# Third attention: scores made a second time by keys, with the row maximum and the mask added by products, and denominators by products with ones

## The chip, the cores and the metric

The kernel is one launch on one core of a Trainium2 chip. The metric is the device time of that launch in microseconds (us); lower is better. The core's engines are TensorE (PE, its weight loads are listed as PEld), VectorE (DVE), ScalarE (ACT), GpSimdE (POOL) and SyncE (SP, which issues transfers). Each works through its own instructions in the order written and waits for others by semaphores.

## What is computed

The reference is a chain of four layers, each an attention between two half-weighted feed-forward parts, on x of 8 batches x 256 tokens x 256 features in fp32. The change touches only the third layer's attention, 32 heads of 8 features each:

```python
q = heads(hidden_states @ wq.T + bq)
k = heads(hidden_states @ wk.T + bk)
v = heads(hidden_states @ wv.T + bv)
scores = jnp.einsum('bhqd,bhkd->bhqk', q, k) / np.sqrt(HD).astype(np.float32)
causal = jnp.tril(jnp.ones((S, S), dtype=bool))
scores = jnp.where(causal, scores, -jnp.inf)
attn = jax.nn.softmax(scores, axis=-1)
out = jnp.einsum('bhqk,bhkd->bhqd', attn, v)
out = out.transpose(0, 2, 1, 3).reshape(B, S, H)
return out @ wo.T + bo
```

## The kernel before

Thirteen stages run one after the other (`STAGES`, L141); the ninth is `attn2`, written once for each engine: `attn2_tensor`, `attn2_scalar`, `attn2_vector`, `attn2_sync` and `attn2_pool`. X, the running sum, stays in SBUF; XTH and XTL are the high and low parts of the normalised, turned input. A product in near-fp32 precision is three fp32r products (`mm3`, L504: high by high, high by low, low by high).

Work goes by batches of 256 tokens (`batch(b)`), batches 1 to 6 in a hardware loop, and inside a batch by the 32 heads in the order `ORDER`, two heads in one step u. For each half of 16 heads, queries and keys are projected to bank 1 (`project`), split into high and low by ACT and DVE (QKH, QKL), and `place` spreads each group of four heads over the partitions: a group's four heads lie in the four 32-row strips, and a product with REP puts high and low parts in 32 rows so that one 32-row product gives a score in the needed precision. Four placements make one half.

For a head, PE makes the scores with queries on the partitions (L2236, L2238): 128 columns for the first 128 queries, 256 for the second; the quarter above the causal diagonal is left out, so a head has TRI = 384 columns. The two heads of a step lie in different strips. DVE adds the mask FMASK, scales and negates, and takes the row minimum (the maximum, negated) in one instruction for each half of the queries (`mask`, L2414); TICK is a marker of one column. ACT makes the exponential with that minimum as bias and sums the row on the way (L2353, L2355) into SUMS. PE turns the three 128 x 128 squares of probabilities (`turn`, L2246), DVE copies them from PSUM to PT (`copy`, L2423), and PE multiplies them by the values (`values`, L2262): VX holds a head's 8 columns of V in 32 columns with zeros around, so four heads that are added up fill a group's 32 rows. `turn` runs LAG = 4 heads behind the scores, `values` four heads at a time behind that. The scores of a step wait until both heads of the step before are masked (banks 4 and 5); SX, PX and PT are rings of 8 heads.

The sums of a half are inverted on DVE (L2399), spread to 8 columns a head by POOL (L2501), turned by PE (L2218), and DVE multiplies the values' products by them (L2404, L2406). ACT and POOL split the result (OTH, OTL), PE projects it (`output`), DVE adds the bias (YO) and POOL adds it to X (L2520). V itself is projected with features on partitions, given its bias by ACT (VT), turned by PE (L2198), copied by DVE (VF) and laid out in VX by POOL.

Of the kernel before, what the change touches and what calls it, by code (L numbers as in the profile page):

```python
# [13 lines left out]
P = 128  # L14
# [39 lines left out]
RING2 = 8  # L54
# [89 lines left out]
def build(nc, d, out):  # L144

    with ExitStack() as ctx:
# [188 lines left out]
        ABIAS = r.put('ABIAS', [P, 3, KC])  # L335
        BO = r.put('BO', [P, D])
        VT = r.put('VT', [P, KC, S])
        FMASK = r.put('FMASK', [P, TRI])
        REPR = r.put('REPR', [P, 4, P])
        REP = r.put('REP', [P, 4, P], F32R)  # L340
        QKH = r.put('QKH', [P, 2, KC, S], F32R)
        QKL = r.put('QKL', [P, 2, KC, S], F32R)
        QKX = r.put('QKX', [P, NG, 2, S], F32R)
        VF = r.put('VF', [P, 2, D])
        VX = r.put('VX', [P, 2, NG, HPG, HPG * HD])
        SX = r.put('SX', [P, RING2, TRI])
        MN = r.put('MN', [P, RING2, 2])
        PX = r.put('PX', [P, RING2, TRI])
        PT = r.put('PT', [P, RING2, TRI])
        TICK = r.put('TICK', [P, NH])  # L350
        SUMS = r.put('SUMS', [P, 2, NH])
        RD = r.put('RD', [P, 2, NH])
        RDX = r.put('RDX', [P, 2, D])
# [36 lines left out]
        def sem(name):  # L390
# [44 lines left out]
        proj_done, qk_high, qk_low, rows_done, rows_sb, v_plus, v_turned, v_sum, v_put = (sem(n) for n in (  # L435
            'proj_done', 'qk_high', 'qk_low', 'rows_done', 'rows_sb', 'v_plus', 'v_turned', 'v_sum', 'v_put'))
        s_done, s_masked, s_exp, s_turned, s_copied, s_pv = (sem(n) for n in (
            's_done', 's_masked', 's_exp', 's_turned', 's_copied', 's_pv'))
        sums_wide, o_kept, o_rd, o_norm, o_turned, o_hi, o_lo, o_done, o_bias = (sem(n) for n in (
            'sums_wide', 'o_kept', 'o_rd', 'o_norm', 'o_turned', 'o_hi', 'o_lo', 'o_done', 'o_bias'))  # L440
# [1720 lines left out]
        LAG = 4  # L2161
        ORDER = [HPC * c + HPG * i + (i + r) % HPG for c in range(KC) for r in range(HPG) for i in range(4)]

        def attn2_tensor(pe, st):
            def project(b, c, parts=(0, 1)):

                tok = at(nc.tensor, b, S, 0)
                if 0 not in parts:
                    pass
                elif c:  # L2170
                    pe.wait_ge(v_sum, at(nc.tensor, b, 1, 1))
                elif not (isinstance(b, int) and b < 2):
                    pe.wait_ge(o_bias, at(nc.tensor, b, 1, -1))
                elif b == 1:
                    pe.wait_ge(qk_low, 4)
                for m in parts:
                    for k in range(KC):
                        col = slice(k * D + c * P, k * D + (c + 1) * P)
                        last = mm3(bank[1][:, m * S:(m + 1) * S], (AWH[:, m, col], AWL[:, m, col]), xt(k, tok, S), k == 0, k == KC - 1)
                if 1 in parts:  # L2180
                    last.then_inc(proj_done, 1)

            def project_values(b, chunks=range(KC)):
                tok = at(nc.tensor, b, S, 0)
                if 0 in chunks:
                    pe.wait_ge(qk_low, at(nc.tensor, b, 4, 2))
                for c in chunks:
                    for k in range(KC):
                        col = slice(k * D + c * P, k * D + (c + 1) * P)
                        last = mm3(bank[1][:, c * S:(c + 1) * S], (AWH[:, 2, col], AWL[:, 2, col]), xt(k, tok, S), k == 0, k == KC - 1)  # L2190
                if KC - 1 in chunks:
                    last.then_inc(proj_done, 1)

            def turn_values(b):
                pe.wait_ge(v_plus, at(nc.tensor, b, 2, 2))
                for t in range(2):
                    for c in range(KC):
                        last = nc.tensor.transpose(bank[1][:, t * D + c * P:t * D + (c + 1) * P], VT[:, c, t * P:(t + 1) * P], ID)  # L2198
                last.then_inc(v_turned, 1)

            def place(b, g):

                if g % 4 == 0:
                    pe.wait_ge(qk_low, at(nc.tensor, b, 4, 2 + g // 2))
                if g or not (isinstance(b, int) and b == 0):
                    pe.wait_ge(rows_sb, at(nc.tensor, b, NG, g))
                rows = slice(32 * (g % 4), 32 * (g % 4) + 32)
                for m in range(2):
                    o = bank[0][:, m * S:(m + 1) * S]
                    nc.tensor.matmul(o, REP[rows, 2 * m, :], QKH[rows, m, g // 4, :], start=True, stop=False)  # L2210
                    last = nc.tensor.matmul(o, REP[rows, 2 * m + 1, :], QKL[rows, m, g // 4, :], start=False, stop=True)
                last.then_inc(rows_done, 1)

            def over_sums(c, count):

                pe.wait_ge(sums_wide, count)
                for t in range(2):
                    last = nc.tensor.transpose(bank[(2, 6)[c]][:, S + t * P:S + (t + 1) * P], RDX[:, t, c * P:(c + 1) * P], ID)  # L2218
                last.then_inc(o_turned, 1)

            def batch(b, prev=True, new=True, following=True):
                n0 = at(nc.tensor, b, NH, 0)

                def scores(u):

                    if 2 * u % HPC == 0:
                        pe.wait_ge(rows_sb, at(nc.tensor, b, NG, NG // KC * (2 * u // HPC + 1)))
                    if prev or u:
                        pe.wait_ge(s_masked, n0 + 2 * u)
                    pair = []  # L2230
                    for n in (2 * u, 2 * u + 1):
                        h = ORDER[n]
                        rows = slice(32 * (h % HPG), 32 * (h % HPG) + 32)
                        pair.append((bank[4 + n % 2], QKX[rows, h // HPG, 0, :], QKX[rows, h // HPG, 1, :]))
                    for o, q, k in pair:
                        nc.tensor.matmul(o[:, 0:P], q[:, 0:P], k[:, 0:P], start=True, stop=True)  # L2236
                    for o, q, k in pair:
                        nc.tensor.matmul(o[:, P:TRI], q[:, P:S], k[:, 0:S], start=True, stop=True).then_inc(s_done, 1)  # L2238

                def turn(h):  # L2240
                    pe.wait_ge(s_exp, n0 + (h + 1))
                    if prev or h >= 2:
                        pe.wait_ge(s_copied, n0 + (h - 1))
                    o = bank[(7, 3)[h % 2]]
                    for n in range(3):
                        last = nc.tensor.transpose(o[:, n * P:(n + 1) * P], PX[:, h % RING2, n * P:(n + 1) * P], ID)  # L2246
                    last.then_inc(s_turned, 1)

                def values(q):

                    if q >= 0 and 4 * q % HPC == 0:
                        pe.wait_ge(v_put, at(nc.tensor, b, 2, 4 * q // HPC + 1))
                        if prev:
                            pe.wait_ge(o_norm, at(nc.tensor, b, 2, 4 * q // HPC - 1))
                    pe.wait_ge(s_copied, n0 + (4 * q + 4))
                    for t, (all_q, cols) in enumerate(((slice(0, S), slice(0, S)), (slice(P, S), slice(S, TRI)))):
                        for n in range(4 * q, 4 * q + 4):
                            h = ORDER[n % NH]
                            c, g, j = h // HPC, h // HPG, h % HPG
                            r = n % HPC // 4  # L2260
                            o = bank[(2, 6)[c]][32 * (g % 4):32 * (g % 4) + 32, 0:S]
                            last = nc.tensor.matmul(o[:, all_q], VX[:, t, g, j, :], PT[:, n % RING2, cols], start=t == 0 and r == 0,  # L2262
                                                    stop=t == 1 and r == HPG - 1)
                    last.then_inc(s_pv, 4)

                def output(t):

                    if t == 0:
                        pe.wait_ge(o_lo, at(nc.tensor, b, 2, 0))
                        if new:  # L2270
                            pe.wait_ge(qk_low, at(nc.tensor, b, 4, 4))
                    for _ in range(1):
                        for c in range(KC):
                            part = slice(t * P, (t + 1) * P)
                            last = mm3(bank[1][:, t * D:(t + 1) * D], (OTH[:, c, part], OTL[:, c, part]),
                                       (AWH[:, 3, c * D:(c + 1) * D], AWL[:, 3, c * D:(c + 1) * D]), c == 0, c == KC - 1)
                    if t:
                        last.then_inc(o_done, 1)
# [667 lines left out]
```

## Time and profile before

| what | value |
|---|---|
| median of 3 runs | 3509.82 us (3506.58 to 3526.61) |
| profiled execution, span | 3445.3 us |
| PE, PEld busy | 2976.1 us (86%), 2582.2 us (75%) |
| DVE, ACT, POOL busy | 2241.7 us (65%), 1565.3 us (45%), 1310.1 us (38%) |
| stage attn2 | 2238.6 to 2656.2 us of the span |

The span goes from the first to the last instruction of the program in the one profiled execution; the time of a run is 64.5 us longer by the median. Busy time of PE contains the latency of each product, so products that follow one another at once overlap in it: a distance from start to start says what a product costs the engine, its duration does not. "Granted clock" (PEclk) is the share of 2.4 GHz that the chip lets TensorE have; it is either all (2.4 GHz) or half (1.2 GHz) at a time, and a stretch's number is the mean.

### The profile page before, as it was taken

What the parts mean: (1) busy time and instruction counts of PE and PEld (TensorE: products, weight loads), DVE (VectorE), ACT (ScalarE), POOL (GpSimd) and SP (SyncE); (2) the same over time, 40 slices, a digit from 0 to 9 for tenths busy, and PEclk for the clock granted to TensorE, in tenths of its full rate; (3) what the DMA queues carried; (4) which work ended last, traced back from release to release, by engine and by line L of the source; (5) the groups of instructions that cost most, each with busy time, mean ns of one, the idle gap of its engine ahead of it and who ended that gap; (6) DMA issues with size and microseconds to landing.
All of it is one profiled execution on the core that took longest, in us unless ns stands there. A gap on an engine that the chain in (4) does not pass through costs nothing.

```text
span 3445.3 us, 59501 instructions
## 1 busy us (share of the span) xinstructions
PE 2976.1 (86%) x19674; PEld 2582.2 (75%) x19674; DVE 2241.7 (65%) x5841; ACT 1565.3 (45%) x3827; POOL 1310.1 (38%) x1254
## 2 busy tenths in 40 slices
PE   8979999999999898895797968488897867977698
PEld 6859989898889787794586957366665766966597
DVE  6756666666666667665636667567887666664755
ACT  3244555555554423334423444366776344433342
POOL 2333444444343405544504455501112454440533
PEclk9989999999999899997898978668998888988899
DMA  2022212121212200331102334400000262330233
GB/s 70 1 72 59 60 48 67 52 67 48 64 52 67 70 10 18 96 111 54 36 0 79 112 118 123 117 4 1 0 0 31 91 164 86 110 89 24 92 96 98
DMA packets 128954, 220.30 MB, mean 64 GB/s; under 512 B 18593, under 2 KB 68001, under 8 KB 128737
## 3 DMA queue, kind: packets, MB, share of 16 engines
q1 hardware_dynamic: 94882, 147.34, 13.7%
q0 software_dynamic: 21216, 57.96, 6.4%
q10 hardware_dynamic: 12672, 12.58, 1.1%
q8 instruction: 111, 1.82, 0.2%
q14 instruction: 73, 0.60, 0.1%
HBM read 170.10 MB, written 47.72 MB: 63 GB/s over the span
## 4 chain that ended last, share of the span: by engine, by line
PE 53%; DVE 16%; issue 12%; POOL 8%; ACT 6%; DMA 4%; DVEq 0%; SPq 0%; POOLq 0%; ACTq 0%
PE bank L507 14%; PE bank L508 13%; PE bank L509 13%; POOL YG L1614 3%; DMA YG<-dyo,POSI 2%; PE bank L2246 2%; POOL HWL L1912 2%; PE bank L1196 2%; PE bank L647 2%; DMA MXG<-dxn,IDX 2%; PE bank L2262 1%; PE bank L1218 1%; POOL KL L1943 1%; DVE DEC L1828 1%; DVE X L1046 1%
## 5 line engine op out<-in xcount | busy, mean ns | idle before, releaser
L1604 POOL DMA_INDIRECT MXG<-dxn,IDX x250 | 236.6, 946 | 315.8 <-PE bank L1196 176.5
L1614 POOL DMA_INDIRECT YG<-dyo,POSI x192 | 188.4, 981 | 168.4 <-DMA dyo<-YS 111.7
L1596 POOL TENSOR_TENSOR MWL<-RAW,MWH 128x608 fp32r<-128x608 f32 (+2 forms) x118 | 179.1, 1526 | 98.5 <-ACT MWH L1299 92.3
L1943 POOL TENSOR_TENSOR QL<-QG,QH 128x512 fp32r<-128x512 f32 x64 | 83.0, 1298 | 249.9 <-ACT QH L1798 249.9
L507 PE MATMUL bank<-MWH,SHH 128*128 128x256 f32 x352 | 110.1, 313 | 72.5 <-DVE SHL L1472 55.2
L2423 DVE COPY PT<-bank 128x384 f32<-128x384 f32 x256 | 132.3, 551 | 60.1 <-PE bank L2246 58.3
L1321 ACT ACTIVATE GH<-bank 128x256 fp32r<-128x256 f32 x250 | 95.9, 384 | 165.8 <-PE bank L1196 165.2
L507 PE MATMUL bank<-MWH,GH 128*128 x500 | 170.7, 341 | 0.0
L671 PE MATMUL bank<-TAB,XN 128*128 128x128 f32 x320 | 60.4, 348 | 118.4 <-ACT XN L592 115.9
L2414 DVE CUSTOM_DVE_ANT_0 SX<-bank,FMASK 128x128 f32<-128x128 f32 (+1 forms) x512 | 152.9, 352 | 12.5 <-issue 11.4
L1912 POOL TENSOR_TENSOR HWL<-RAW,HWH 128x640 fp32r<-128x640 f32 x68 | 113.2, 1676 | 120.1 <-DVE DEC L1829 119.9
L1018 POOL TENSOR_TENSOR HL<-HID,HH 128x512 fp32r<-128x512 f32 x56 | 72.4, 1293 | 226.1 <-ACT HH L985 225.7
L507 PE MATMUL bank<-XTH,WH 128*128 128x512 f32 (+1 forms) x384 | 153.7, 400 | 4.0 <-DVE HF L1029 2.3
L509 PE MATMUL bank<-MWH,GL 128*128 x500 | 154.9, 310 | 0.0
L508 PE MATMUL bank<-MWL,GH 128*128 x500 | 154.7, 309 | 0.0
L508 PE MATMUL bank<-XTL,WH 128*128 128x512 f32 (+1 forms) x384 | 151.2, 394 | 0.0
L509 PE MATMUL bank<-XTH,WL 128*128 128x512 f32 (+1 forms) x384 | 150.5, 392 | 0.0
L507 PE MATMUL bank<-MH,XTH 128*128 128x256 f32 x512 | 148.9, 291 | 1.1 <-DVE ML L1864 1.1
L2353 ACT ACTIVATE PX<-SX,MN 128x128 f32<-128x128 f32 x256 | 101.2, 395 | 101.6 <-DVE MN L2414 99.6
L1535 DVE TENSOR_TENSOR GL<-bank,GH 128x256 fp32r<-128x256 f32 x250 | 105.8, 424 | 62.4 <-ACT GH L1321 60.5
L509 PE MATMUL bank<-MH,XTL 128*128 128x256 f32 x512 | 145.3, 284 | 0.0
L508 PE MATMUL bank<-ML,XTH 128*128 128x256 f32 x512 | 145.1, 283 | 0.0
(449 smaller groups left out, 11388.1 us busy)
## 6 DMA issues: line engine op xcount, KB each, us to landing
dyo<-YS SPq DMA_DIRECT2D x250, 128.0 KB
RAW<-in_wheads SPq DMA_DIRECT2D x68, 320.0 KB, 6.0
RAW<-in_eL SPq DMA_DIRECT2D x64, 304.0 KB, 2.8
BB<-dgates SPq DMA_DIRECT2D x68, 256.0 KB, 3.5
GB<-dgates SPq DMA_DIRECT2D x68, 256.0 KB, 4.2
dxn<-XN ACTq DMA_DIRECT2D x16, 512.0 KB, 4.4
RAW<-in_eL SPq DMA_DIRECT2D x32, 256.0 KB, 2.7
RAW<-in_sL SPq DMA_DIRECT2D x18, 384.0 KB, 3.0
```

Source lines behind the costliest of these rows:

```text
L507: nc.tensor.matmul(o, lh, rh, start=start, stop=False)
L508: nc.tensor.matmul(o, lh, rl, start=False, stop=False)
L509: return nc.tensor.matmul(o, ll, rh, start=False, stop=stop)
L1535: nc.vector.tensor_tensor(GL[:, b % DEEP, :], bank[X_BANK[b % 2]][:, 0:D], f32(GH[:, b % DEEP, :]), ALU.subtract).then_inc(b_xlo, 1)
L1596: nc.gpsimd.tensor_tensor(MWL[:, at_:at_ + cols], RAW[:, n % RAW_SLOTS, 0:cols], f32(MWH[:, at_:at_ + cols]), ALU.subtract).then_inc(w_rea ...
L1604: nc.gpsimd.indirect_dma_start(MXG[:, n % XGS, :], None, dxn, bass.IndirectOffsetOnAxis(ap=IDX[:, b:b + 1], axis=0)).then_inc(x_in[n % XGS ...
L1614: nc.gpsimd.indirect_dma_start(YG[:, i % YGS, :], None, dyo[0:m.blocks * P, :], bass.IndirectOffsetOnAxis(ap=POSI[:, c * NT + t:c * NT + t ...
L1912: nc.gpsimd.tensor_tensor(HWL[:, parity, part], RAW[:, slot, 0:PIECE], f32(HWH[:, parity, part]), ALU.subtract).then_inc(w_ready, 1)
L1943: nc.gpsimd.tensor_tensor(lo[:, :], src[:, :], f32(hi[:, :]), ALU.subtract).then_inc(qk_ready, 1)
L2353: nc.scalar.activation(PX[:, a, 0:P], SX[:, a, 0:P], ACT.Exp, scale=-1.0, bias=MN[:, a, 0:1], accum_out=SUMS[:, 0, h:h + 1])
L2414: last = nc.vector.tensor_tensor_reduce(out=SX[:, h % RING2, part], in0=bank[4 + h % 2][:, part], in1=FMASK[:, part], scale=-float(HD) ** ...
L2423: nc.vector.tensor_copy(PT[:, h % RING2, :], bank[(7, 3)[h % 2]][:, 0:TRI]).then_inc(s_copied, 1)
```

## The change

The loop over batches is written out, and all engines run through one counter n from -20 to 280 (`ALL2`), one head a step. Scores with queries on the partitions are still made and masked (`by_queries`, `mask`), but only for the row extremes: unscaled, with the masked scores going to a scratch ring SX of two. For eight heads at a time DVE splits the negated maxima into a high and a low part (`split_least`, MNX), PE turns them (`turn_least`, three 128 x 128 squares) and ACT copies them to MROW, where they are rows. Twelve heads behind, PE makes the scores again with keys on the partitions (`by_keys`): REP by MROW puts the negated maximum of each query on all key partitions, LATER by TWOID (bf16) adds the mask, and two products of keys by queries add the scores, all in one of three banks (3, 7, 6). ACT makes one exponential of 384 columns from PSUM straight into PT, without a sum. PE multiplies PT by VX and, into the other half of bank 2, by ONEX, which has ones where VX has values, so that the denominators come out already in place; DVE inverts them (128 x 256) and multiplies.

V is projected with tokens on the partitions, so it isn't turned; its bias is added on DVE. PX, the turns, the copies, SUMS, RD, POOL's spreading and the turns of the sums are gone. PT is a ring of 12 heads, QKX holds three halves. Bank 1 is shared by projections, V, outputs and turned minima in one fixed order (`BANK1`). At the start ONEX and MNX are cleared and ones set, and LATER and TWOID are made.

```diff
-                def scores(u):
-                    if prev or u:
-                        pe.wait_ge(s_masked, n0 + 2 * u)
...
-                    for o, q, k in pair:
-                        nc.tensor.matmul(o[:, 0:P], q[:, 0:P], k[:, 0:P], start=True, stop=True)
-                    for o, q, k in pair:
-                        nc.tensor.matmul(o[:, P:TRI], q[:, P:S], k[:, 0:S], start=True, stop=True).then_inc(s_done, 1)
-
-                def turn(h):
-                    pe.wait_ge(s_exp, n0 + (h + 1))
...
-                    for n in range(3):
-                        last = nc.tensor.transpose(o[:, n * P:(n + 1) * P], PX[:, h % RING2, n * P:(n + 1) * P], ID)
+            def by_queries(n):
+                half, i, j, s = head_at(n)
...
+                if n >= 2:
+                    pe.wait_ge(s_masked, n - 1)
...
+                nc.tensor.matmul(o[:, 0:P], q[:, 0:P], k[:, 0:P], start=True, stop=True)
+                nc.tensor.matmul(o[:, P:TRI], q[:, P:S], k[:, 0:S], start=True, stop=True).then_inc(s_done, 1)
+
+            def turn_least(k):
+
+                pe.wait_ge(least_in, k + 1)
+                pe.wait_ge(one_free, BANK1['least', k])
+                for n, t in enumerate((0, 1, 1)):
+                    last = nc.tensor.transpose(bank[1][:, n * P:(n + 1) * P], f32(MNX[:, k % 2, t, :]), ID)
+                last.then_inc(least_turned, 1)
+
+            def by_keys(n):
+                half, i, j, s = head_at(n)
+                if n % 8 == 0:
+                    pe.wait_ge(one_free, BANK1['least', n // 8] + 1)
+                if n >= len(PB):
+                    pe.wait_ge(s_exp, n - len(PB) + 1)
...
+                nc.tensor.matmul(o[:, 0:TRI], REP[rows, 4 + s, :], MROW[rows, n // 8 % 3, :], start=True, stop=False)
+                early = o[:, 0:TRI].rearrange('p (a q) -> p a q', q=P)[:, 0:3:2, :]
+                nc.tensor.matmul(early, LATER[:, :], TWOID[:, :, :], start=False, stop=False)
+                nc.tensor.matmul(o[:, 0:S], k[:, 0:P], q[:, 0:S], start=False, stop=False)
+                nc.tensor.matmul(o[:, S:TRI], k[:, P:S], q[:, P:S], start=False, stop=True).then_inc(b_scores, 1)
+
+            def values(quad):
...
+                pe.wait_ge(s_exp, 4 * quad + 4)
+                for lo, left in ((0, lambda t, i, j: VX[:, t, 4 * c + i, j, :]), (S, lambda t, i, j: ONEX[:, j, :])):
...
+            for n in ALL2:
+                if 0 <= n < HEADS:
+                    by_queries(n)
+                if of_oct(n, 9) is not None:
+                    turn_least(of_oct(n, 9))
...
+                if 0 <= n - BEHIND < HEADS:
+                    by_keys(n - BEHIND)
+                if 0 <= n - LATE < HEADS and (n - LATE) % QUAD == 0:
+                    values((n - LATE) // QUAD)
...
+            def exp(n):
+                act.wait_ge(b_scores, n + 1)
+                if n >= RING2:
+                    act.wait_ge(s_pv, n - RING2 + 1)
+                nc.scalar.activation(PT[:, n % RING2, :], bank[PB[n % len(PB)]][:, 0:TRI], ACT.Exp, scale=float(HD) ** -0.5).then_inc(s_exp, 1)
...
-                def copy(h):
...
-                    nc.vector.tensor_copy(PT[:, h % RING2, :], bank[(7, 3)[h % 2]][:, 0:TRI]).then_inc(s_copied, 1)
...
+            def norm(half):
+                dve.wait_ge(s_pv, HPC * (half + 1))
...
+                step(nc.vector.reciprocal(RDX[:, :], bank[2][:, S:2 * S]))
+                nc.vector.tensor_tensor(ON[:, c, :], bank[2][:, 0:S], RDX[:, :], ALU.mult).then_inc(o_norm, 1)
```

On PE, in the steady part of a batch, four heads before (L2236 and L2238 are scores, L2246 turns, L2262 values):

```order
L2262 MATMUL bank<-PT,VX 32x256 x4
L2262 MATMUL bank<-PT,VX 32x128 x4
L2246 MATMUL bank<-TAB,PX 128x128 x6
L2236 MATMUL bank<-QKX 128x128 x2
L2238 MATMUL bank<-QKX 128x256 x2
L2246 MATMUL bank<-TAB,PX 128x128 x6
L2236 MATMUL bank<-QKX 128x128 x2
L2238 MATMUL bank<-QKX 128x256 x2
```

and now one head and a half there with a group of values (L2250 and L2251 are scores by queries, L2270 to L2274 the scores by keys):

```order
L2250 MATMUL bank<-QKX 128x128
L2251 MATMUL bank<-QKX 128x256
L2270 MATMUL bank<-MROW,REP 128x384
L2272 MATMUL bank<-TWOID,LATER 128x2x128
L2273 MATMUL bank<-QKX 128x256
L2274 MATMUL bank<-QKX 128x128
L2289 MATMUL bank<-PT,VX 32x256 x4
L2289 MATMUL bank<-PT,VX 32x128 x4
L2289 MATMUL bank<-PT,ONEX 32x256 x4
L2289 MATMUL bank<-PT,ONEX 32x128 x4
L2250 MATMUL bank<-QKX 128x128
L2251 MATMUL bank<-QKX 128x256
```

Turns have left the row, scores stand head by head instead of in pairs, and the second making of the scores, with its full product L2272 between 32-row ones, and eight products with ONEX have come in. On DVE two heads before (L2423 copies turned probabilities, L2414 masks):

```order
L2423 COPY PT<-bank 128x384 x2
L2435 MEMSET TICK 128x1
L2414 ISA SX,MN<-bank,FMASK 128x128
L2414 ISA MN 128x1
L2414 ISA SX,MN<-bank,FMASK 128x256
L2414 ISA MN 128x1
L2435 MEMSET TICK 128x1
L2414 ISA SX,MN<-bank,FMASK 128x128
L2414 ISA MN 128x1
L2414 ISA SX,MN<-bank,FMASK 128x256
L2414 ISA MN 128x1
```

and now at the place where a half's sums are inverted (L2392 masks):

```order
L2392 ISA SX,MN<-bank,FMASK 128x128
L2392 ISA MN 128x1
L2392 ISA SX,MN<-bank,FMASK 128x256
L2392 ISA MN 128x1
L2412 RECIPROCAL RDX<-bank 128x256
L2413 TENSOR_TENSOR ON<-bank,RDX 128x256
L2392 ISA SX,MN<-bank,FMASK 128x128
L2392 ISA MN 128x1
```

The masks follow one another without copies between them, and once in sixteen heads a reciprocal of 256 columns stands in the row.

## Rows read from the trace of the kernel before

**Rows 1.** The page's first part: busy time, share and instructions of each engine.

```profile
PE 2976.1 (86%) x19674; PEld 2582.2 (75%) x19674; DVE 2241.7 (65%) x5841; ACT 1565.3 (45%) x3827; POOL 1310.1 (38%) x1254
```

**Rows 2.** Table by stretches: length, busy time of each engine, granted clock, DMA.

```profile
2238.60:2656.20 417.60, 367.97 (x3008) 267.70 (x3008) 315.03 (x1632) 292.10 (x1154) 50.28 (x104) 0.84 0.00 1
2256.00:2304.00 48.00, 45.18 (x292) 33.65 (x292) 33.66 (x183) 33.52 (x131) 1.41 (x3) 0.66 0.00 1
2448.00:2496.00 48.00, 42.59 (x381) 30.94 (x380) 39.35 (x207) 36.01 (x144) 6.31 (x13) 0.93 0.00 0
```

**Rows 3.** Chain of waits in order of time: start, length, what.

```profile
2466.57 1.44 PE bank L2262 x16
...
2514.32 1.44 PE bank L2262 x16
```

**Rows 4.** Order of time on PE at full clock: start, duration, instruction.

```profile
2410.53 0.33 PE L2238 MATMUL bank<-QKX 32*128 32x256 f32 x2
2410.80 0.39 PE L507 MATMUL bank<-XTH,AWH 128*128 x1
2411.02 0.28 PE L508 MATMUL bank<-XTL,AWH 128*128 x1
2411.14 0.27 PE L509 MATMUL bank<-XTH,AWL 128*128 x1
...
2411.48 0.28 PE L509 MATMUL bank<-XTH,AWL 128*128 x1
2411.61 0.82 PE L2246 MATMUL bank<-TAB,PX 128*128 128x128 f32 x6
2412.35 0.33 PE L2236 MATMUL bank<-QKX 32*128 32x128 f32 x2
...
2412.78 0.38 PE L507 MATMUL bank<-XTH,AWH 128*128 x1
...
2413.68 0.86 PE L2262 MATMUL bank<-PT,VX 128*32 128x256 f32 x16
2414.47 0.87 PE L2246 MATMUL bank<-TAB,PX 128*128 128x128 f32 x6
2415.27 0.33 PE L2236 MATMUL bank<-QKX 32*128 32x128 f32 x2
```

**Rows 5.** Waits from 2256 to 2645: total, times, longest.

```profile
PEld bank L2236 <- DVE MN L2414: 27.1, 56, 0.8
```

**Rows 6.** Groups from 2256 to 2645: busy us, mean ns, idle before.

```profile
L2423 DVE COPY PT<-bank 128x384 f32<-128x384 f32 x253 | 130.7, 551 | 59.5 <-PE bank L2246 57.8
...
L2355 ACT ACTIVATE PX<-SX,MN 128x256 f32<-128x256 f32 x256 | 127.0, 496 | 0.0
L2353 ACT ACTIVATE PX<-SX,MN 128x128 f32<-128x128 f32 x256 | 101.2, 395 | 101.6 <-DVE MN L2414 99.6 <-PE bank L2246 2.0
```

**Rows 7.** Order of time on DVE: two heads masked.

```profile
2401.78 0.28 DVE L2414 CUSTOM_DVE_ANT_0 SX<-bank,FMASK 128x128 f32<-128x128 f32 x1
...
2402.34 0.28 DVE L2414 CUSTOM_DVE_ANT_0 SX<-bank,FMASK 128x128 f32<-128x128 f32 x1
```

**Rows 8.** A reciprocal of 256 columns in another stage, durations min/median/max.

```profile
L2116 DVE RECIPROCAL DEN<-DEN x16: 1753/1753/1754, 1628.8 to 1677.0; 128x256 f32<-128x256 f32 x16
```

**Rows 9.** PE at the stage's start, the first scores and the last values.

```profile
2238.59 0.55 PE L507 MATMUL bank<-XTH,AWH 128*128 128x256 f32 x1 [8.81 <-POOL AWL L2744]
...
2255.92 0.47 PE L2236 MATMUL bank<-QKX 32*128 32x128 f32 x2 [0.69 <-ACT QKX L2338]
...
2647.74 0.86 PE L2262 MATMUL bank<-PT,VX 128*32 128x256 f32 x16 [0.79 <-DVE PT L2423]
```

**Rows 10.** PE at the half level of the clock.

```profile
2326.44 1.54 PE L2246 MATMUL bank<-TAB,PX 128*128 128x128 f32 x6
2327.91 0.47 PE L2236 MATMUL bank<-QKX 32*128 32x128 f32 x2
...
2328.63 0.58 PE L507 MATMUL bank<-AWH,OTH 128*128 128x256 f32 x1
```

More of the change, by code:

```diff
@@ new lines, in build, with head_at, rows_at, of_half @@
+        HALVES2 = 2 * B
+        HEADS = HPC * HALVES2
+        ORDER = [HPG * i + (i + r) % HPG for r in range(HPG) for i in range(4)]
+        BEHIND, LATE, QUAD = 12, 19, 4
+        OCTS = HEADS // 8
+        PB = (3, 7, 6)
+        def head_at(n):
+            half, m = divmod(n, HPC)
+            h = ORDER[m]
+            return half, h // HPG, h % HPG, m // 4 % 2
+        def rows_at(half, i):
+            return half % 3 * 4 + i
+        def of_half(n, first):
+            half, rest = divmod(n - first, HPC)
+            return half if rest == 0 and 0 <= half < HALVES2 else None
@@ new lines, in output @@
+            def output(b, t):
+                if t == 0:
+                    pe.wait_ge(o_lo, 2 * b + 2)
+                    pe.wait_ge(one_free, BANK1['output', b])
+                for c in range(KC):
+                    part = slice(t * P, (t + 1) * P)
+                    last = mm3(bank[1][:, t * D:(t + 1) * D], (OTH[:, c, part], OTL[:, c, part]),
+                               (AWH[:, 3, c * D:(c + 1) * D], AWL[:, 3, c * D:(c + 1) * D]), c == 0, c == KC - 1)
+                if t:
+                    last.then_inc(o_done, 1)
@@ L2309, in attn2_tensor @@
             pe.wait_ge(xt_lo, (st.tr + 1) * HALF)
             pe.wait_ge(w_ready, st.pieces + 4)
[L2311 to L2321 removed]
+            pe.wait_ge(prepared, 17)
@@ L2372, in attn2_scalar, with rows @@
-            act.wait_ge(ld_c, 240)
-            high(0, 0)
-            values(0)
-            for g in range(4):
-                rows(0, g)
-            batch(0, prev=False)
-            with act.Fori(1, B - 1) as i:
-                batch(i)
-            batch(B - 1, following=False)
-            batch(B, new=False, following=False)
+            def rows(half, i):
+                act.wait_ge(rows_done, 4 * half + i + 1)
+                nc.scalar.activation(QKX[:, rows_at(half, i), :, :], bank[0][:, :].rearrange('p (m t) -> p m t', m=2), ACT.Copy).then_inc(rows_sb, 1)
@@ new lines, in attn2_scalar @@
+            act.wait_ge(ld_c, 256)
+            for n in ALL2:
+                if of_oct(n, 9) is not None:
+                    least_high(of_oct(n, 9))
+                if of_half(n, -18) is not None:
+                    high(of_half(n, -18))
+                for i in range(4):
+                    if of_half(n, 2 * i - 12) is not None:
+                        rows(of_half(n, 2 * i - 12), i)
+                if 0 <= n - BEHIND < HEADS:
+                    exp(n - BEHIND)
+                if of_half(n, 34) is not None:
+                    result(of_half(n, 34))
@@ new lines, in attn2_vector @@
+            nc.vector.tensor_copy(LATER[:, :], FMASK[:, 0:P]).then_inc(prepared, 1)
+            nc.vector.tensor_copy(TWOID[:, :, :], TAB[:, 0:1, :].to_broadcast([P, 2, P])).then_inc(prepared, 1)
+            for n in ALL2:
+                if 0 <= n < HEADS:
+                    mask(n)
+                if of_oct(n, 7) is not None:
+                    split_least(of_oct(n, 7))
+                if of_half(n, -17) is not None:
+                    low(of_half(n, -17))
+                if of_batch(n, 6) is not None:
+                    keep_values(of_batch(n, 6))
+                if of_half(n, 33) is not None:
+                    norm(of_half(n, 33))
+                if of_batch(n, 54) is not None:
+                    over(of_batch(n, 54))
```

458 lines of the change are left out of this document (172 added, 286 removed).

## The prediction

> **What bounds the kernel now.** I read the page first, then the stretches of the third attention (L2 attention, lines 2160 to 2520), then the order of time of one engine at a time. The page gives a span of 3445.3 us with PE the busiest engine [rows 1]. The table by stretches [rows 2] cuts out the stage: from PE's first product at 2238.6 to the last addition into X at 2656.2, 417.6 us, with PE busy 368 of them, DVE 315 and ACT 292. Only this stage is changed; everything before and after keeps its work, so the question is what happens to these 417.6 us.
>
> A batch has 32 heads and in steady state takes 47.75 us: the chain of waits has the same group of values' products at 2466.57 and at 2514.32 [rows 3]. Of 48 us PE is busy 42.6 and DVE 39.4 [rows 2]. "Busy" on PE counts the latency of the last product, so I rebuilt PE's own work from start-to-start distances at the full clock [rows 4], at places where nothing waits:
> - a pair of heads' scores: 2412.35 to 2412.78, 0.43 us. The rows are x2: the two heads use different 32-row strips of the array and run at the same time;
> - six turns of probabilities and the way back to the next scores: 2414.47 to 2415.27, 0.80;
> - four heads' values (x16, since each fp32 product is two passes): 2413.68 to 2414.47, 0.79;
> - six products of a projection: 2412.78 to 2413.68, 0.90;
> - one placement, four 32-row products of 256 columns: at the regular spacing of 0.12 (2411.02 to 2411.14) 0.5.
> Per batch: 16 x 1.23 + 8 x 0.79 + 8 x 0.90 + 8 x 0.5 + 8 small turns of 0.11 = 38 us. The other 10 us are waiting and half clock. The idle times show a ring between two engines: DVE's copy of turned probabilities waits for PE's turn, 57.8 us over the stage [rows 6], and PE's scores wait for DVE's masking, 27.1 [rows 5]. So now neither PE nor DVE is full; they take turns.
>
> **What the change takes away.** DVE loses the 256 copies of 0.55 us (131 us of the stage) and 256 markers of one column. ACT's two exponentials, 0.395 and 0.496 us, each with a read of its sum, become one of 384 columns without a sum, 0.395 + 2 x 0.10 = 0.60 us, an estimate from the 128- and 256-column rows [rows 6]. DVE per batch after: 32 maskings of 0.56 (2401.78 to 2402.34) [rows 7], two reciprocals of 256 columns at 1.75 [rows 8], and some 6 us of small work: 27 us. ACT: 32 x 0.60, 8 row copies of 0.58, the rest 5: 29 us. Both are then far from binding, so the ring is gone and PE alone sets the pace.
>
> **What it does to PE.** The 768 turns go: 0.80 a pair, 0.40 a head. In comes, per head, a second making of the scores. The important thing in the row-by-row view is what a change between 32-row products and products over the whole array costs. From the first of them [rows 4]: the pair's 256-column products start at 2410.53, the first full product at 2410.80, 0.27 later, of which the columns are 0.11 (the regular spacing 2411.02 to 2411.14 being 0.12): 0.16 to leave. The first full product then holds the second until 2411.02, 0.22 in place of 0.12: 0.10 for the first weights. Back to 32 rows: 2411.61 to 2412.35 is 0.74, six turns are 0.65 of it: 0.09. A wait between two full products costs none of this (2411.48 to 2411.61 is regular). The Trainium skill says the same in "TensorEngine Tiling (Array Packing)", Key Properties: changing the mode, not only the tile, drains the engine; the trace agrees, with 0.16 and 0.09 us, and the rule speaks against this change, which does it twice more per head.
>
> In the new order by_keys is a 32-row product (REP by MROW, 384 columns), a full one (LATER by TWOID, 256), then two 32-row ones (256 and 128). by_queries now stands singly. Start to start at full clock:
> 1. the two query products one after the other in one strip: between 0.05 (columns only) and 0.16 [rows 4]; I take 0.10.
> 2. REP by MROW lies in the neighbouring strip and can start beside them, so 384 columns, 0.16, plus 0.13 of the way out of 32 rows: 0.29. If it does not overlap, 0.11 more.
> 3. LATER: 0.22 as a first full product plus 0.09 back: 0.31.
> 4. the 256-column key product as a first one: 0.22; the 128-column one 0.05 to 0.16, I take 0.09.
> Sum 1.01 us a head; with the lower ends 0.92, with all the upper ones 1.25. Before, scores and turns were 0.615.
>
> Values: the products with ONEX double the stream. Columns alone are 2 x 0.22 + 2 x 0.11 = 0.66 a quad, so 0.79 becomes 1.45, plus 0.1 to come from 32 rows: 1.55. Turning the minima: three products between 32-row ones, 0.27 + 0.38 + 0.05 = 0.7, four times a batch. Projections, now always between 32-row products, 0.90 + 0.12. Placement 0.5. Not needed any more: turns of V and of sums, counted above.
> Per batch: 32 x 1.01 + 8 x 1.55 + 4 x 0.7 + 8 x 1.02 + 8 x 0.5 = **59.7 us**, against 47.8 now. Every wait I can name is shorter than two steps of 1.9 us: masking 0.56 behind a two-bank ring, exponential 0.60 behind three banks, reciprocal and product 2.2 with two steps before the next half's values. What is queued behind the reciprocal on DVE is the masking of the next head, and PE asks for that two heads later.
>
> **The sum.** Fill: today 17.3 us from 2238.6 to the first scores [rows 9]; the values' projection now comes later, so 12.5. Eight batches: 478. The first 12 heads run without by_keys at the pace of the masking, +5. Tail after the last values: 2647.74 [rows 9] to 2656.2 today, 9 with the long reciprocal. Together 504 against 417.6: **+87 us at full clock**.
> Clock: at the half level (1.2 GHz) the same steps take 0.72 for 0.43 and 1.47 for 0.74 [rows 10], so about 1.8 times; time spent there does 0.55 of its work. Now the steady batches are granted 0.93 of the clock and the first 0.66 [rows 2]. At 0.93, a seventh of the time at the half level, the 478 would become 510, +32; at 1.00 nothing. PE no longer pauses for DVE, but 32-row products fill little of the array; I take 15.
> Stage +102, so the profiled span should be near 3547 and the time, counted from the median of the runs, 3509.8 + 102 = **3612 us**. Profiled span and median differ by 65 us of work outside the span, which the change leaves.
> Low end of this case: 0.92 a head (-23) and no loss (-15): 3574. High end: 1.25 a head (+61) and a granted 0.93 (+17): 3690.
>
> **Rivals.**
> - *Full clock throughout.* The stretches at the half level now hold turns, and if turns do not hold the clock up, taking them out gives back 15: 3597. Against it: the six turns at 2411.61 run at 0.11 each, at 2.4 GHz, and the batch at 2448, with its full share of turns, has the grant of 0.93, the first batch, whose turns begin only after four heads, 0.66 [rows 2]. The Trainium skill, "TensorE: Matmul & The Clock Gate", Part 4, says that transposes do not engage the full clock; by it this rival, with 15 less, would be the sum, and the trace does not settle it.
> - *The clock stays low.* Between two values' bursts the new order has some 4 us with only a quarter of the array in most products. The first batch ran at a granted 0.66 although PE was busy 45.2 of 48 us [rows 2]. At 0.66 throughout, 478 becomes 1 / (1 - 0.68 x 0.45) = 1.44 times as much, +210; at 0.80 it is +105. On top of the 3597 at full clock: 3702 to 3807, middle 3750. It decides over the forecast from about 0.86 down (+69).
> - *Faster: the changes of tiling are hidden.* If weights are loaded ahead and the 32-row and full products follow without a gap, a head is columns only, 0.05 + 0.16 + 0.11 + 0.11 + 0.05 = 0.5, values 1.4, a projection 0.75: 16 + 11.2 + 2 + 6 + 4 = 39 us a batch, 314 + 27 = 341 for the stage, 3433. The point from which it decides is 0.61 us a head; below it the change is faster. The rows speak against it at each of the changes that they show [rows 4]; what it has for it is that no row shows a bf16 product between 32-row ones. Half hidden, 0.65 to 0.8 a head: 3520 to 3560.
> - *Nothing moves,* because DVE's relief is eaten by another wait: only by chance, since no engine's sum comes to 47.8.
>
> **Chances.** Forecast 0.57 (3574 to 3690); full clock throughout 0.15 (3574 to 3650); low clock 0.14; half hidden 0.07; hidden 0.07. More than 0.5% faster (below 3492) 0.07, within 0.5% (about what a measurement of this kernel tells from no change) 0.03, slower 0.90. The range leaves out the hidden case and the upper part of the low clock: 3535 to 3710.
>
> **What would show it.** Right: PE's busy share of the stage over 95%, DVE near 27 and ACT near 29 us a batch, no wait of PE for masking; LATER's product 0.25 to 0.30 after REP's and the key product 0.3 after that; a batch of 58 to 63 us; stage near 520. Wrong if: the distance over by_keys is below 0.5 us (hidden); the granted clock in the stage is below 0.86 (low); or PE waits for MROW, for the exponentials or for bank 1, which would be a ring that I took to be slack.

## The result and the profile after

The changed kernel takes 3805.8 us (median of 4 runs) where the kernel before, run beside it, takes 3518.2: 1.082 times as long, 95% interval 1.077 to 1.087. Forecast were 3612 and a range up to 3710. The direction was right; the loss is 288 us where 102 were expected.

Nearly all of it lies in the stage. The table by stretches of the changed kernel (length, busy time of each engine, granted clock, DMA), first the stage, then two pieces of its middle, which answers to [rows 2]:

```profile
2274.90:2971.50 696.60, 684.59 (x4320) 454.82 (x4320) 232.67 (x1169) 199.40 (x402) 40.17 (x88) 0.59 0.01 1
2400.00:2500.00 100.00, 100.00 (x607) 66.33 (x608) 30.68 (x156) 26.33 (x53) 5.56 (x12) 0.55 0.00 1
2800.00:2900.00 100.00, 100.00 (x710) 66.43 (x702) 35.82 (x185) 31.30 (x64) 6.17 (x15) 0.65 0.00 1
```

The stage has grown from 417.6 to 696.6 us, +279. In its middle PE is busy for 100.00 of 100 us, DVE and ACT for about a third: the ring between PE and DVE is gone, as forecast, and PE alone is the bound. But the granted clock is 0.59 where it was 0.84 in the stage before and up to 0.93 in its middle.

The waits, which answer to [rows 5] and [rows 6], have turned round; total, times, longest:

```profile
DVE SX L2392 <- PE bank L2251: 421.6, 222, 5.9
ACT PT L2350 <- PE bank L2274: 335.5, 230, 6.1
```

Order of time on PE (start, duration, instruction), at a place where the clock goes from the full to the half level; it answers to [rows 4] and [rows 10]. L2250 and L2251 are the scores by queries, L2270 is REP by MROW, L2272 LATER by TWOID, L2273 and L2274 keys by queries. The one full product of a head, over all 128 rows, is L2272; the others lie in one 32-row strip, and going from the one kind to the other is called a change of tiling:

```profile
2484.27 0.28 PE L2272 MATMUL bank<-TWOID,LATER 128*128 128x256 bf16 x1
...
2485.13 0.55 PE L2258 MATMUL bank<-TAB,MNX 128*128 128x128 f32 x3
2485.61 0.43 PE L2270 MATMUL bank<-MROW,REP 32*128 32x384 f32 x1
2485.98 0.28 PE L2272 MATMUL bank<-TWOID,LATER 128*128 128x256 bf16 x1
2486.19 0.38 PE L2273 MATMUL bank<-QKX 32*128 32x256 f32 x1
2486.20 0.43 PE L2270 MATMUL bank<-MROW,REP 32*128 32x384 f32 x1
2486.41 0.22 PE L2274 MATMUL bank<-QKX 32*128 32x128 f32 x1
2486.47 0.27 PE L2250 MATMUL bank<-QKX 32*128 32x128 f32 x1
2486.58 0.33 PE L2251 MATMUL bank<-QKX 32*128 32x256 f32 x1
2486.84 0.39 PE L2272 MATMUL bank<-TWOID,LATER 128*128 128x256 bf16 x1
...
2488.31 0.39 PE L2272 MATMUL bank<-TWOID,LATER 128*128 128x256 bf16 x1
```

A head at the full level is one LATER product to the next: 2485.98 to 2486.84, 0.86 us. The next head, at the half level, is 2486.84 to 2488.31, 1.47 us. A head with turned minima takes 2484.27 to 2485.98, 1.71, so these cost 0.85. Projection and values, at the full level:

```profile
2389.97 0.28 PE L2272 MATMUL bank<-TWOID,LATER 128*128 128x256 bf16 x1
...
2392.11 0.28 PE L2272 MATMUL bank<-TWOID,LATER 128*128 128x256 bf16 x1
...
2392.98 0.28 PE L2272 MATMUL bank<-TWOID,LATER 128*128 128x256 bf16 x1
...
2393.56 0.86 PE L2289 MATMUL bank<-PT,VX 128*32 128x256 f32 x16
2394.24 0.83 PE L2289 MATMUL bank<-PT,ONEX 128*32 128x256 f32 x16
...
2395.42 0.28 PE L2272 MATMUL bank<-TWOID,LATER 128*128 128x256 bf16 x1
```

The first pair is a head with a projection, 2.14, the last a head with four heads' values, 2.44: 1.28 and 1.58 more than a bare head. A batch at the full level is thus 32 x 0.86 + 8 x 1.58 + 8 x 1.28 + 4 x 0.85 = 54 us, and the stage 458, with 26 us of fill, start and tail taken over from the forecast. The grant gives the same from the other side: at 0.59, 0.82 of the time is at the half level, where work takes 1.47 for 0.86, so 696.6 us are worth 460 at the full level.

So the 279 us are two parts: +40 of work at the full level, and **+239 because TensorE ran most of the stage at 1.2 GHz**. That is the arithmetic; whether what PE does is the cause of the clock, and which part of it, is what the runs below are for. In them the stage is compared, since what lies outside it is the same work and differs from one set of runs to another (below).

### The profile page after: what moved, and what is told of

Its sections match the earlier page's. It is cut to its first block, busy times and chain, and to the rows that moved or that the text cites. A ratio compares the mean times of both kernels' runs of the same rounds, so it can differ in the third digit from the quotient of the medians.

```text
span 3794.3 us, 59343 instructions
## 1 busy us (share of the span) xinstructions
PE 3305.1 (87%) x20986; PEld 2773.5 (73%) x20986; DVE 2153.0 (57%) x5385; ACT 1464.8 (39%) x3075; POOL 1301.9 (34%) x1238
## 4 chain that ended last, share of the span: by engine, by line
PE 61%; DVE 14%; issue 9%; POOL 6%; ACT 5%; DMA 2%; another core or an unknown queue 2%; SPq 0%; POOLq 0%; DVEq 0%; ACTq 0%
PE bank L506 14%; PE bank L508 12%; PE bank L507 12%; PE bank L2289 4%; PE bank L2273 3%; PE bank L2272 2%; PE bank L2270 2%; PE bank L2251 2%; POOL HWL L1911 2%; PE bank L1195 2%; PE bank L2250 1%; PE bank L646 1%; PE bank L1217 1%; POOL KL L1942 1%
## 5 line engine op out<-in xcount | busy, mean ns | idle before, releaser
L2392 DVE CUSTOM_DVE_ANT_0 SX<-bank,FMASK 128x128 f32<-128x128 f32 (+1 forms) x512 | 161.8, 356 | 422.8 <-PE bank L2251 421.6
L2350 ACT ACTIVATE PT<-bank 128x384 f32<-128x384 f32 x256 | 125.8, 491 | 336.9 <-PE bank L2274 335.5
L2270 PE MATMUL bank<-MROW,REP 32*128 32x384 f32 x256 | 154.6, 604 | 0.0
L506 PEld LDWEIGHTS bank<-MWH,SHH 128*128 128x128 f32 x352 | 72.0, 205 | 111.1 <-DVE SHL L1471 73.6
```

The costliest lines, as they stand in the source:

```text
L506: nc.tensor.matmul(o, lh, rh, start=start, stop=False)
L2270: nc.tensor.matmul(o[:, 0:TRI], REP[rows, 4 + s, :], MROW[rows, n // 8 % 3, :], start=True, stop=False)
L2350: nc.scalar.activation(PT[:, n % RING2, :], bank[PB[n % len(PB)]][:, 0:TRI], ACT.Exp, scale=float(HD) ** -0.5).then_inc(s_exp, 1)
L2392: last = nc.vector.tensor_tensor_reduce(out=SX[:, n % 2, part], in0=bank[4 + n % 2][:, part], in1=FMASK[:, part], scale=-1.0, scalar=3e38, ...
```

## Experiments

**The kernel before, and the changed one, again.**

> The kernel before, unchanged, for a second profile. The first one has a span of 3445.3 us while the median of the runs is 3518. If the span is simply the run's time (as in the changed kernel, 3794.3 for 3796.1), this profile should have a span within 2 us of its run, near 3510, with the stage attn2 again near 418 us and the difference of 60 us in the mixture-of-experts stages outside it. If instead some 65 us lie outside the span in every run, the span is again near 3445.

Measured: span 3440.8 us, median 3439.4; stage 408.6.

> The changed kernel once more, beside the kernel before on the same chip, as the base for the other runs of this set. The ratio should again be 1.08, with a granted clock near 0.59 in the stage.

Measured: 1.0845 (1.0799 to 1.089), stage 718.7 us at a grant of 0.56. The first expectation met neither of its cases: span and run agree within 2 us, but both are near 3440, not 3510. The same program takes 3434 to 3445 us in some sets of runs and 3518 in others. The first profile of before (span 3445.3) is at the one level, the median counted from (3509.8) at the other, so the 64.5 us "outside the span" don't exist. Outside the stage, the traces sum to 3013 to 3032 us in the one and 3097 to 3104 in the other. Why is open; different chips are a guess that the runs don't settle. after, after_again, noones and both fillers were taken at the 3518 level, all others at the lower one, so their times are compared only as ratios to the kernel before beside them.

**More work of one kind.** Edits to `by_keys`, in later2 (later4 has 4), and in rep2:

```diff
-                nc.tensor.matmul(early, LATER[:, :], TWOID[:, :, :], start=False, stop=False)
+                for _ in range(2):
+                    nc.tensor.matmul(early, LATER[:, :], TWOID[:, :, :], start=False, stop=False)
```
```diff
-                nc.tensor.matmul(o[:, 0:TRI], REP[rows, 4 + s, :], MROW[rows, n // 8 % 3, :], start=True, stop=False)
+                for stop in (True, False):
+                    nc.tensor.matmul(o[:, 0:TRI], REP[rows, 4 + s, :], MROW[rows, n // 8 % 3, :], start=True, stop=stop)
```

> The changed kernel with the product LATER by TWOID made twice, so 256 more columns over the whole array per head (a mask added twice does the same). Theory clock: the stage is long because its 32-row products leave TensorE at the half level (granted 0.59); full-array work brings the full level back. The added columns cost 0.11 us a head at the full level, 28 in all, but with a grant over 0.85 the stage should be near 520 in place of 697 and the time near 3640. Rival work: PE is full and the granted clock has another cause than what PE does; then the added columns cost 0.11 to 0.21 us for 256 heads, +28 to +54, and the time is 3835 to 3860.

> The changed kernel with the product REP by MROW made twice (384 more columns in one 32-row strip per head, the first result thrown away). If full-array work is what counts for the clock, as against PE being busy, the grant stays at 0.55 to 0.62 and the time rises by 0.16 to 0.32 us for 256 heads, to 3850 to 3890. If any added column counts, the grant rises above 0.8 and the time falls below 3750.

> The changed kernel with the product LATER by TWOID made four times, 768 columns over the whole array more than in the changed kernel, without a further change of tiling. In later2 one more product took the stage from 697 to 587 us and the grant from 0.59 to 0.79. Theory clock: the grant goes on to 0.95 or more; then the stage is the full-level sum of the changed kernel, 8 x 54 + 27 = 460, plus 3 x 0.12 x 256 = 92, some 550 to 570, still shorter than with one. Rival (one product was a lucky place between two levels): the added 0.24 to 0.38 us a head make it 650 or more.

The stage of each, later2, later4, then rep2, in the table by stretches:

```profile
2235.80:2822.80 587.00, 574.70 (x4576) 372.54 (x4576) 231.97 (x1168) 198.68 (x402) 40.20 (x88) 0.79 0.01 2
```
```profile
2234.80:2790.50 555.70, 543.49 (x5088) 374.49 (x5088) 233.13 (x1168) 197.81 (x402) 40.13 (x88) 0.96 0.01 2
```
```profile
2235.80:2998.20 762.40, 750.46 (x4576) 492.11 (x4576) 233.85 (x1168) 199.39 (x402) 40.02 (x88) 0.55 0.01 1
```

Work that is thrown away makes the stage *shorter*: 697 to 719 us without it, 587 with one more full product a head, 556 with three (the whole kernel 1.055, 1.048 to 1.063, and 1.042, 1.038 to 1.045, of the kernel before, where the changed kernel is 1.082 to 1.0845). The grant goes from 0.56 to 0.59 over 0.79 to 0.96. later4 lies where the full-level sum put it, 550 to 570. So the clock does follow what PE does. PE was 100% busy from 2400 to 2500 in all of them, so being busy is not enough, and rep2, run beside later2, shows that 384 columns in a 32-row strip don't help: 762 us at 0.55. Its bare head, from LATER to LATER (L2273 there), still takes 0.86 at the full level, the doubled product running beside those of the other strip:

```profile
2492.45 0.28 PE L2273 MATMUL bank<-TWOID,LATER 128*128 128x256 bf16 x1
2493.31 0.28 PE L2273 MATMUL bank<-TWOID,LATER 128*128 128x256 bf16 x1
```

**Less of one kind.** `noones` leaves out the products with ONEX (the denominators).

> The changed kernel without the products with ONEX (left out: the denominators; the values' products are divided by themselves). They are a burst of column-tiled work over all 128 rows, 0.66 us per four heads at the full level. Theory by columns: at a grant of 0.59 the stage loses 64 x about 1.2 us, near 75, and the time falls to about 0.98 of the changed kernel's. Theory clock: with this dense burst gone the rest sits even more at the half level (0.50 to 0.55), so that less comes back, 30 to 60 us.

```profile
2272.90:2970.70 697.80, 685.87 (x3296) 455.24 (x3296) 233.72 (x1168) 200.35 (x402) 39.98 (x88) 0.51 0.00 1
```

1024 records fewer on PE (3296 for 4320), and the stage takes 698 us, against 719 in after_again beside it and 697 in the first profile: the grant fell from 0.56 to 0.51 and took most of what the columns gave back. The median is 18 us lower (1.081 of the kernel before, 1.077 to 1.085, against 1.0845), short even of the 30 us expected. At this clock the denominators by products with ones, taken alone, cost at most about 20 us of the 75 that their columns would.

**Turns against products.** Both fillers stand ahead of REP by MROW, into the bank that it overwrites; fill_masks, and in fill_turns in its place `nc.tensor.transpose(o[:, part], FMASK[:, 0:P], ID)` for two parts:

```diff
+                for _ in range(2):
+                    nc.tensor.matmul(o[:, 0:S], LATER[:, :], TWOID[:, :, :].rearrange('p a q -> p (a q)'), start=True, stop=True)
```

> The changed kernel with two turns (128 x 128, fp32) ahead of each head's REP by MROW, into the bank that this then overwrites. They cost two more changes of tiling and 0.22 us a head at full clock, 0.43 at half. If turns hold the clock up as other full-array products do, the grant rises as in fill_masks and the two times are within 30 us of one another. If turns don't count for the clock, the grant stays near 0.59 and this run is over 100 us slower than fill_masks.

> The same place and the same columns' time as fill_turns, but two bf16 products of 256 columns over the whole array in place of the turns. Theory clock: 512 more full-array columns a head bring the grant over 0.85 although two changes of tiling come with them, and the stage is no longer than the changed kernel's 697 us, about 600.

```profile
2272.50:3188.40 915.90, 903.94 (x4832) 569.74 (x4832) 231.21 (x1168) 199.97 (x402) 39.96 (x88) 0.58 0.00 1
```
```profile
2277.20:3207.20 930.00, 918.09 (x4832) 549.68 (x4832) 231.09 (x1168) 200.65 (x402) 40.04 (x88) 0.56 0.00 1
```

First fill_turns, then fill_masks. The two agree within 15 us, as the case in which turns count had it. But the test is weak: neither filler raised the grant above that of the kernel without one, so it doesn't tell whether turns would hold it up where other full products do. Both expectations for fill_masks were wrong: 512 more full columns a head, twice what helped in later2, and the grant stays at 0.56, the stage is 930 us. What differs from later2 is where they stand: between 32-row products, with two more changes of tiling. That pointed to the changes of tiling; the runs that follow test it.

**Without the mask product.** `nomask` leaves LATER by TWOID out (the causal mask in the second scores).

> The changed kernel without LATER by TWOID (left out: the causal mask in the second scores; the exponential's scale is made small so that it stays finite). All products of a head are then 32-row ones: the two changes of tiling a head are gone with the 256 full columns. Theory clock and tiling: the grant falls to 0.50 to 0.53, and yet a head falls from 1.47 to some 0.95 us at the half level, so the stage is 560 to 600. If the changes of tiling cost nothing and only columns count, it loses 0.21 a head, and the stage is 640 to 660.

```profile
2236.40:2602.90 366.50, 339.79 (x4064) 268.39 (x4064) 225.63 (x1168) 180.05 (x402) 40.29 (x88) 0.91 0.01 3
```

The expectation on the clock was plainly wrong, 0.91 where at most 0.53 was expected, and the stage is 367 us, *shorter than before the change*. Hardly any full product is left in a head, and the clock is up. In the order of time on PE:

```profile
2521.09 0.27 PE L2272 MATMUL bank<-QKX 32*128 32x256 f32 x1
2521.09 0.44 PE L2270 MATMUL bank<-MROW,REP 32*128 32x384 f32 x1
2521.20 0.22 PE L2273 MATMUL bank<-QKX 32*128 32x128 f32 x1
2521.26 0.28 PE L2250 MATMUL bank<-QKX 32*128 32x128 f32 x1
2521.37 0.33 PE L2251 MATMUL bank<-QKX 32*128 32x256 f32 x1
2521.37 0.28 PE L2272 MATMUL bank<-QKX 32*128 32x256 f32 x1
```

A head is 2521.09 to 2521.37, 0.28 us in place of 0.86 (0.29 is usual among the stage's bare heads): with nothing full between them the strips run at the same time, and the two makings of the scores overlap. The two runs that tell the columns of the mask from its changes of tiling; touch adds to nomask

```diff
+                nc.tensor.matmul(o[:, 0:16], LATER[:, :], TWOID[:, 0, 0:16], start=False, stop=False)
```

and mask32 uses `LATER[rows, :], TWOID[rows, :, :]` for all 256 columns.

> nomask with a product over the whole array of only 16 columns where LATER by TWOID stood (left out: the rest of the mask; the exponential's scale is small). It brings back the two changes of tiling a head, and next to no columns. If the changes of tiling alone thin out the work and let the clock fall, the grant is 0.50 to 0.56 and the stage, 367 us in nomask, is 600 to 670. If it was the 256 columns of the mask that cost, the stage stays under 420 at a grant over 0.85.

> The changed kernel with LATER by TWOID cut to the head's own 32 rows (left out: three quarters of the mask; the exponential's scale is small), so 256 columns as before and no change of tiling. If the changes of tiling are the cause, the stage is 367 us as in nomask plus up to 0.11 us for 256 heads, 370 to 400, at a grant over 0.85. If 32-row columns in themselves pull the clock down, the grant is under 0.65 and the stage over 550.

```profile
2234.70:2859.00 624.30, 611.86 (x4320) 432.76 (x4320) 233.38 (x1169) 196.64 (x402) 40.19 (x88) 0.63 0.01 2
```
```profile
2233.50:2682.20 448.70, 427.10 (x4320) 325.88 (x4320) 228.28 (x1168) 184.02 (x402) 40.29 (x88) 0.78 0.01 2
```

touch, first: sixteen full columns a head, and the stage goes from 367 to 624 us, as expected, the grant from 0.91 to 0.63, not quite as low as the 0.50 to 0.56 expected. mask32, second, without the changes, is 449 at 0.78, between its two cases: with 256 more columns in the strip the grant is lower than in nomask. The changes of tiling are the larger cause, 258 us against 82. Neither number is the clock's alone. A bare head of touch at the full level, from L2271 to L2271:

```profile
2598.90 0.18 PE L2271 MATMUL bank<-TWOID,LATER 128*128 128x16 bf16 x1
2599.66 0.18 PE L2271 MATMUL bank<-TWOID,LATER 128*128 128x16 bf16 x1
```

That is 0.76 us, 0.47 more than in nomask, where 0.16 + 0.09 for the two changes would be 0.25; the rest is that the strips no longer run side by side. An estimate from these: 0.47 for 256 heads is 120 of the 258 us, and the clock the other half. Which part of a change lowers the clock, the gap itself or the lost overlap, these runs don't separate.

**Half as many changes.** In `pairs` both makings of the scores take two heads at a time: both REP products, both LATER products, both first key products, both second ones; the scores by queries in pairs as in the kernel before.

```diff
+                for o, rows, s, q, k in pair:
+                    nc.tensor.matmul(o[:, 0:TRI], REP[rows, 4 + s, :], MROW[rows, n // 8 % 3, :], start=True, stop=False)
+                for o, rows, s, q, k in pair:
...
+                    nc.tensor.matmul(early, LATER[:, :], TWOID[:, :, :], start=False, stop=False)
```

> The changed kernel with two heads at a time in both makings of the scores: the two heads' 32-row products stand next to one another in different strips, the two LATER products between them, so half as many changes of tiling. Theory clock and tiling: at the full level a head falls from the 0.865 us measured in the changed kernel to about 0.55, at the half level from 1.473 to about 0.95, and full-array columns come closer together, so the grant rises too. With the grant still at 0.6 the stage loses 0.4 us for 256 heads, some 100, time near 3700; with a grant over 0.85 it is near 400 and the time near 3520. Rival (the products do not overlap across strips and only the columns count): no more than 30 us faster.

> The order in pairs again, as a base for the next run on the same chip: stage near 402 us, grant near 0.91, time 0.994 of the kernel before.

```profile
2234.40:2628.30 393.90, 371.14 (x4320) 253.08 (x4320) 226.25 (x1168) 186.44 (x402) 40.33 (x88) 0.93 0.01 2
2400.00:2500.00 100.00, 98.38 (x1215) 66.84 (x1210) 63.37 (x329) 51.46 (x114) 11.26 (x26) 1.00 0.01 2
```

These rows are of pairs_again, the stage and a piece of its middle: 394 us, and a grant of 1.00 in the middle. In pairs the stage was 402. The same products as in the changed kernel, in another order, take some 300 us less in the stage, and the whole kernel goes from 1.082 to 0.994 of the kernel before. This is the strongest of the runs: no work is added or left out, only the order differs. Against the kernel before, the time is 0.994 in both runs (0.991 to 0.997; 0.992 to 0.997): **this version beats both**, by 0.6%. It is even better than the 3520 expected, seen as a ratio (1.000).

**Fewer changes still.** `pairs_joined` runs projections, outputs and turned minima between the REP and the LATER products of the next pair.

> The order in pairs, and every group of full-array products (projections, outputs, turned minima) moved between the REP by MROW and the LATER products of the next pair, where the tiling changes anyway. Twelve groups a batch then need no change of their own. Theory tiling: 0.25 us each, 3 us a batch, 24 in all, so 1.3% under the kernel before: stage near 380. If waits of these groups (for bank 1, for split minima) come to stand in front of the scores by keys, up to 20 us of it are lost.

```profile
2234.40:2651.40 417.00, 377.75 (x4320) 260.95 (x4320) 227.53 (x1168) 178.92 (x402) 40.38 (x88) 0.89 0.01 2
```

It failed: ratio 1.000 (0.998 to 1.002), stage 417 at a grant of 0.89. PE now waits for the exponentials ahead of the held-back groups; total, times, longest, from 2300 to 2600:

```profile
PE bank L2276 <- ACT PT L2366: 6.9, 25, 0.3
PEld bank L2276 <- ACT PT L2366: 11.9, 25, 0.5
PEld bank L2252 <- DVE MN L2408: 10.3, 25, 0.6
```

In pairs_again the first two are missing there, and the last is 3.0. The first two are the same waits, seen at the product and at its weight load, so they don't add up: some 19 us more waiting in these 300. The grant fell besides, from 0.93 to 0.89. How the 23 us by which the stage is longer, and the gain that didn't come, divide between the two is not shown.

## Why the prediction was wrong

- **PE becomes the bound, the ring goes away**: right. PE 100% busy in the middle, DVE 233 and ACT 199 us of 697: 29 and 25 us a batch, forecast 27 and 29. ACT was put too high by the exponential, 0.49 us and not 0.60:

```profile
L2350 ACT ACTIVATE PT<-bank 128x384 f32<-128x384 f32 x256 | 125.8, 491 | 336.9 <-PE bank L2274 335.5
```

- **The changes of tiling cost time at each head**: right in kind. 0.16 and 0.09 us were read correctly from [rows 4], and come back as 0.15 and 0.10 in the changed kernel (2486.58 to 2486.84 and 2485.98 to 2486.19, less 0.11 for 256 columns). touch and nomask show that the changes decide the stage, by more than these two numbers.
- **The sum at full clock**: somewhat too high, 59.7 us a batch forecast, 54 measured. Terms: a head 1.01 forecast, 0.86 measured (the bf16 LATER product is followed by the key product after 0.21, not 0.31; a 128-column product in the strip takes 0.06, not 0.09); values 1.55 against 1.58; projection 1.02 against 1.28; turned minima 0.7 against 0.85; a placement runs beside other strips and costs 0.03, where 0.5 was taken. Net -46 us of 478, so +40 instead of +87.
- **The clock**: this is the step that failed. "I take 15" was a number between 0 and 32, from the grants 0.93 and 1.00. It is 239: the stage ran at a grant of 0.59, and later2, later4 and pairs show that the order and kind of PE's own products set it, with PE 100% busy in the middle of the first two and 98% in pairs. The prediction set "PE no longer pauses" against "32-row products fill little of the array" and took a term between the two, with no row behind it. The row that spoke against it was in [rows 2]: busy 45.2 of 48 us at a grant of 0.66. The rival *the clock stays low* has the result, but its number is luck: at 0.66 it gave 3807, measured 3806 at 0.59, its full-level sum and its grant being too high by amounts that cancel. It had 0.14, and the range cut off its upper part. Its mechanism, a quarter of the array in most products, holds only in part: nomask has nearly nothing but 32-row products in a head and runs at 0.91, with the strips side by side. What goes with the low clock in these runs is 32-row products that stand alone between full ones; the changes of tiling had been priced for their gaps, not for this.
- **The range** was built around one level of the clock. The steps take 1.7 times as long at the other, so a case that leans on the clock has two outcomes far apart.
- *Full clock throughout* falls: with the turns out, the grant went from 0.84 to 0.59. The Trainium skill's sentence in "TensorE: Matmul & The Clock Gate", Part 4, that transposes do not engage the full clock, stays undecided: turns do run at the full level among other work, 0.11 us each [rows 4], and fill_turns has a grant of 0.58 where fill_masks has 0.56, but no run here has a place where other full products raise the clock and turns take their place.
- *Changes of tiling hidden* falls by the 0.86 us a head. Its 0.5 us a head by columns alone is not a lower bound: without LATER's 0.11 it would be 0.39, and nomask takes 0.28, as strips overlap.

## What to carry to other kernels

Before writing small-row products and full ones in turn, count the changes between them: each cost 0.1 to 0.2 us by itself here, kept the strips from running side by side, and came with a low clock, at which everything takes 1.7 times as long. Group products of one tiling over two or more heads first; and if a stage is 100% busy at half clock, one wasted full product next to an existing full one is a quick test of whether the clock follows what PE does there. A forecast in which PE becomes the bound needs two sums, one at each level, and both belong in the range.

## What the hardware showed that was not expected

- A stage of 700 us with PE 100% busy in its middle at a grant of 0.59, which gets 141 us shorter (697 to 556) by 768 more columns a head.
- Columns left out that give back 20 us at most where 75 were to be had by columns (noones), since the clock takes the rest.
- Products of another strip start ahead of their turn: REP at 2486.20 before L2274 at 2486.41, which stands ahead of it in the program and has its own strip and bank.
- The same program differs by some 80 us between sets of runs (3434 to 3445 and 3518 us), outside this stage. The stage itself differs by 22 us between two profiles of the changed kernel at the same level (697 and 719), with the grant (0.59 and 0.56). Times are only compared with those of a base that ran beside them.
